# Scaling after the experts instead of before: rounded parts of x1, tokens on partitions, in a one-core MetaFormer block

## The reference

```
x = x + attention(layernorm_over_channels(x))          # x: 8 images, 128 channels, 48*48 tokens
t = tokens of x                                        # 128 channels each
logits = layernorm(t) @ gate_w + router_gamma
combine = softmax(logits), only the two largest of 8 kept
mod[e] = gam[e] * (layernorm(t) @ expert_w[e] + expert_b[e]) + bet[e]
t = t + sum over e of combine[e] * mod[e]
```

## Time and profile before

| | |
|---|---|
| median of three runs (lowest to highest) | 736.78 us (733.86 to 740.26) |
| profiled execution, its own time | 737.64 us |
| its span, first to last instruction | 735.9 us |
| busy TensorE / weight loads / VectorE | 681.8 / 458.9 / 632.3 us |
| busy ScalarE / GpSimd | 292.0 / 468.7 us |
| mean granted TensorE clock | 0.978 |

### The profile page before, as it was taken

The page is one execution under the profiler, slowest core; times in us unless marked ns, Lnnn a source line. Parts: engine busy times, 40 slices in busy tenths (PEclk is TensorE's granted clock), DMA queues, the critical chain, the costliest instruction groups (busy, mean ns, idle before and its releaser), DMA issues.

```text
span 735.9 us, 35372 instructions
## 1 busy us (share of the span) xinstructions
PE 681.8 (93%) x13757; PEld 458.9 (62%) x13865; DVE 632.3 (86%) x1690; ACT 292.0 (40%) x865; POOL 468.7 (64%) x696
## 2 busy tenths in 40 slices
PE   3667999989999999999999999999999999999986
PEld 1656656656666666666666666666666666665542
DVE  3667999988999999999999999999999999988762
ACT  1134434433444444444444444444444444434311
POOL 5365765565667676767676767676767676764521
PEclk9788999999999999999999999999999999999997
DMA  4111111111111111111111111111111111011000
GB/s 109 53 35 32 45 32 46 46 45 32 45 43 43 43 43 43 43 43 43 43 43 42 44 42 43 42 44 42 44 42 43 42 43 41 29 31 33 17 17 29
DMA packets 60229, 30.53 MB, mean 41 GB/s; under 512 B 2160, under 2 KB 60176, under 8 KB 60176
## 3 DMA queue, kind: packets, MB, share of 16 engines
q1 hardware_dynamic: 60176, 29.79, 14.2%
HBM read 20.34 MB, written 9.44 MB: 40 GB/s over the span
## 4 chain that ended last, share of the span: by engine, by line
PE 82%; issue 8%; POOL 4%; DVE 4%; DMA 1%; ACT 1%; SPq 0%; DVEq 0%; POOLq 0%; ACTq 0%
PE bank_o L1134 31%; PE num L1048 7%; PE num L1031 5%; PE wide_a L1128 4%; PE wide_a L1000 3%; PE num L1015 3%; PE bank_g L1071 3%; PE bank_g L960 3%; PE bank_g L911 3%; PE bank_g L1086 2%; PE bank_g L975 2%; PE wide_a L943 2%; PE bank_o L1093 2%; PE wide_a L945 2%; PE wide_b L943 2%
## 5 line engine op out<-in xcount | busy, mean ns | idle before, releaser
L1134 PE MATMUL bank_o<-xs,e_w 128*128 128x512 f32 x576 | 279.7, 610 | 0.2 <-DVE xs L774 0.2
L1134 PEld LDWEIGHTS bank_o<-xs,e_w 128*128 128x128 f32 x576 | 99.3, 191 | 88.0 <-issue 87.5
L338 POOL TENSOR_TENSOR qn<-feat,rden 128x512 f32<-128x512 f32 x36 | 38.8, 1077 | 114.0 <-DVE rden L654 114.0
L374 POOL TENSOR_TENSOR xs<-spread,x 128x1024 f32<-128x1024 f32 x36 | 97.7, 2714 | 4.4 <-ACT spread L498 4.4
L774 DVE TENSOR_TENSOR xs<-wide_a,x 128x1024 f32<-128x1024 f32 x72 | 87.5, 1215 | 6.2 <-PE wide_b L1128 6.1
L456 ACT ACTIVATE q_eo<-bank_g,parity 128x512 f32<-128x512 f32 x72 | 45.5, 683 | 96.3 <-PE bank_g L975 96.3
L465 ACT ACTIVATE squares<-bank_g 128x128 f32<-128x128 f32 x108 | 28.5, 274 | 137.3 <-issue 70.0
L326 POOL TENSOR_TENSOR k_sum<-k_sum,feat 128x64 f32<-128x64 f32 x216 | 68.8, 318 | 16.9
L637 DVE SCALAR_TENSOR_TENSOR feat<-ex,qkv 128x512 f32<-128x512 f32 x72 | 79.3, 1103 | 0.0
L366 POOL TENSOR_TENSOR coef<-weight,coef 128x256 fp32r<-128x256 f32 x36 | 26.1, 724 | 83.0 <-ACT coef L486 83.0
L307 POOL TENSOR_TENSOR x_low<-x,x_high 128x512 fp32r<-128x512 f32 x36 | 61.1, 1697 | 4.6 <-ACT x_high L421 4.6
(11 more groups left out here) (161 smaller groups left out, 1630.7 us busy)
## 6 DMA issues: line engine op xcount, KB each, us to landing
x<-in_x SPq DMA_DIRECT2D x36, 256.0 KB, 2.9
x_res<-in_x SPq DMA_DIRECT2D x36, 256.0 KB, 2.9
...
```

The lines of the kernel that those rows point to most:

```text
L374: tt(xs[:, g.par, 2 * pair:2 * pair + 2], spread[:], flat(x1[:, g.par]).unsqueeze(1) .broadcast_to([128, 2, U * T]), ALU.mult).then_inc(S[ ...
L1134: last = mm(bank_o[:], e_w[:, e], xs[:, g.par, e], start=False, stop=(final and e % 2 == 1), skip_group_check=True)
```

## The change

The experts no longer read scaled copies of `x1`. ScalarE rounds `x1` to `x1_high`, GpSimd takes the rest `x1_low`, and `experts(g, u, half)` makes, for one image and four experts, three fp32r matmuls of 512 columns with the tokens as the stationary operand: the result has tokens on partitions and four experts side by side in a bank. Since tokens are on partitions, an expert's weight for a token is a per-partition scalar: ScalarE scales experts 5 to 8 into `part` (`scaled_by_scalar`), GpSimd adds these in pairs to `two_sums` (`add_parts`), and VectorE multiplies and adds experts 1 to 4 onto the first sum in `total` (`experts_1_to_4`). TensorE's `output` puts the bias rows, the transposed `two_sums` and the transposed `total` into `bank_o`. One transpose of `pack` replaces four of `coef4`. `spread_scales`, `scale_pair`, `spread_pair`, `sel` and `e_w` are gone; the expert weights are centred and split (`e_high`, `e_low`).

The set-up is cut up: the first images are transposed ahead of `first_weights`, and the rest of it stands inside the first steps (`if first(g)`). GpSimd's fills of `v_pad`, `state` and others pass to VectorE. SyncE loads the second images ahead of the small weights, stores at age 9 instead of 7 and loads the residual at age 4 instead of 3. The steps of all engines are in a new order.

The core of the diff:

```diff
+        weight = sb("weight", [128, U, EXPERTS])
+        scale = sb("scale", [128, PAR, U, EXPERTS])
+        pack = sb("pack", [128, U, 2, 2, EXPERTS], F32R)
         coef_t = sb("coef_t", [128, PAR, U * T], F32R)
-        spread = sb("spread", [128, 2, 512])
-        xs = sb("xs", [128, PAR, EXPERTS, U * T])
+        part = sb("part", [128, U, 4, 128])
+        two_sums = sb("two_sums", [128, PAR, U, 2, 128])
+        total = sb("total", [128, PAR, U, 128])
         o = sb("o", [128, PAR, U, T])
...
                 g = at(0)
                 if g:
                     load_later(g)
-                g = at(7)
+                g = at(9)
                 if g:
                     store(g)
-                g = at(3)
+                g = at(4)
                 if g:
                     load_residual(g)
 
-            steps(sp, step, 7)
...
+            def x1_low_part(g):
+                need(pool, "x1_high_done", g.i + 1)
+                need(pool, "a_2", g.i - 1)
+                tt(x1_low[:, g.par], x1[:, g.par], x1_high[:, g.par].bitcast(F32), ALU.subtract)\
+                    .then_inc(S["x1_low_done"], 1)
+
+            def add_parts(g, p):
+                need(pool, f"part{2 * p}", g.i + 1)
+                need(pool, f"part{2 * p + 1}", g.i + 1)
                 need(pool, "out_done", g.i - 1)
-                tt(xs[:, g.par, 2 * pair:2 * pair + 2], spread[:], flat(x1[:, g.par]).unsqueeze(1)
-                   .broadcast_to([128, 2, U * T]), ALU.mult).then_inc(S[done], 1)
+                two = slice(2 * p, 2 * p + 2)
+                tt(two_sums[:, g.par, two], part[:, two, 0:2], part[:, two, 2:4], ALU.add).then_inc(S[f"two_sums{p}"], 1)
...
+            def x1_high_part(g):
+                need(act, "x1_done", g.i + 1)
+                need(act, "a_2", g.i - 1)
+                need(act, "x1_low_done", g.i - 1)
+                nc.scalar.activation(x1_high[:, g.par], x1[:, g.par], copy).then_inc(S["x1_high_done"], 1)
+
+            def scaled_by_scalar(g, u):
+                need(act, "scale_done", g.i + 1)
+                need(act, f"two_sums{u // 2}", g.i)
+                need(act, f"b_{u}", g.i + 1)
+                for e in range(4):
+                    last = nc.scalar.activation(part[:, u, e], w_bank[B_BANK[u]][:, 128 * e:128 * e + 128], copy,
+                                                scale=scale[:, g.par, u, 4 + e:5 + e])
+                last.then_inc(S[f"part{u}"], 1)
...
-                nc.scalar.activation(spread[:].rearrange("p n t -> p (n t)"), bank[:], copy).then_inc(S[done], 1)
+                need(act, "out_done", g.i - 1)
+                for u in range(U):
+                    rows = slice(ROWS * u, ROWS * u + ROWS)
+                    last = nc.scalar.activation(coef_t[rows, g.par, T * u:T * u + T], bank_g[rows, 0:T], copy)
...
+            def expert_weights():
                 for e in range(EXPERTS):
-                    make(nc.vector.tensor_scalar(e_w[:, e], w_bank[e // 4][:, 128 * (e % 4):128 * (e % 4) + 128],
-                                                 gamma_all[:, e:e + 1], None, ALU.mult))
-                dve.wait_ge(S["rest_pe"], 3)
-                make(stt(e_bias[:], e_bias_raw[:], gamma_col[:], num[0:EXPERTS, 256:384], ALU.mult, ALU.add))
-                dve.wait_ge(S["rest_pe"], 4)
-                make(copy(eb_high[:], num[:, 640:768]))
-                dve.wait_ge(S["rest_dve"], done[0])
-                make(tt(eb_low[:], num[:, 640:768], eb_high[:].bitcast(F32), ALU.subtract))
-                dve.wait_ge(S["rest_dve"], done[0])
-                make(tt(eb_rows[:], num[:, 512:640], eb_low[:], ALU.add))
-                assert done[0] == REST_DVE
-                dve.wait_ge(S["rest_dve"], REST_DVE)
+                    make(nc.vector.tensor_scalar(e_high[:, e], e_centred[:, e], gamma_all[:, e:e + 1], None, ALU.mult))
+                dve.wait_ge(S["rest_dve"], BIASES + EXPERTS)
+                for e in range(EXPERTS):
+                    make(stt(e_low[:, e], e_centred[:, e], gamma_all[:, e:e + 1], e_high[:, e].bitcast(F32),
+                             ALU.mult, ALU.subtract))
...
-                tt(weight[:, :, 0], weight[:, :, 1], per_token(rstd2[:, g.par]), ALU.mult).then_inc(S["scale_done"], 1)
-
-            def scale_pair(g, pair, spread_done, done):
-                need(dve, spread_done, g.i + 1)
-                need(dve, "x1_done", g.i + 1)
+                need(dve, "part0", g.i - 1)
+                need(dve, "part1", g.i - 1)
+                need(dve, "part2", g.i - 1)
+                need(dve, "part3", g.i - 1)
+                tt(scale[:, g.par], weight[:], per_token(rstd2[:, g.par]), ALU.mult).then_inc(S["scale_done"], 1)
+
+            def experts_1_to_4(g, p):
                 need(dve, "out_done", g.i - 1)
-                tt(xs[:, g.par, 2 * pair:2 * pair + 2],
-                   (wide_a, wide_b)[pair % 2][:].rearrange("p (n t) -> p n t", n=2),
-                   flat(x1[:, g.par]).unsqueeze(1).broadcast_to([128, 2, U * T]), ALU.mult).then_inc(S[done], 1)
+                need(dve, f"two_sums{p}", g.i + 1)
+                need(dve, "scale_done", g.i + 1)
+                need(dve, f"a_{2 * p}", g.i + 1)
+                need(dve, f"a_{2 * p + 1}", g.i + 1)
+                done = S[f"a_steps{p}"]
+                for e in range(4):
+                    for k in range(2):
+                        u = 2 * p + k
+                        if e > 0:
+                            dve.wait_ge(done, 6 * g.i + 2 * e - 1 + k)
+                        before = total[:, g.par, u] if e > 0 else two_sums[:, g.par, u, 0]
+                        last = stt(total[:, g.par, u], w_bank[A_BANK[u]][:, 128 * e:128 * e + 128],
+                                   scale[:, g.par, u, e:e + 1], before, ALU.mult, ALU.add)
+                        if e < 3:
+                            last.then_inc(done, 1)
+                last.then_inc(S[f"a_sum{p}"], 1)
 
...
+                    features(g, 0)
+                    if first(g):
+                        gammas_and_gate()
 
             first_weights()
-            rest_of_weights()
             steps(dve, step, 6)
...
+            def experts(g, u, half):
+                if first(g):
+                    pe.wait_ge(S["rest_dve"], REST_DVE)
+                need(pe, "x1_low_done", g.i + 1)
+                if (u, half) == (0, 0):
...
-                    last = mm(bank_o[:], e_w[:, e], xs[:, g.par, e], start=False, stop=(final and e % 2 == 1),
+                        need(pe, "a_sum1", g.i)
+                        need(pe, "part3", g.i)
+                out, four = w_bank[(A_BANK, B_BANK)[half][u]], slice(4 * half, 4 * half + 4)
+                mm(out, x1_high[:, g.par, u], e_high[:, four], start=True, stop=False)
+                mm(out, x1_high[:, g.par, u], e_low[:, four], start=False, stop=False)
+                mm(out, x1_low[:, g.par, u], e_high[:, four], start=False, stop=True).then_inc(S[f"{'ab'[half]}_{u}"], 1)
+
+            def output(g):
+                if first(g):
+                    pe.wait_ge(S["rest_dve"], REST_DVE)
+                need(pe, "a_sum0", g.i + 1)
+                need(pe, "a_sum1", g.i + 1)
+                need(pe, "squares_done", g.i + 2)
+                need(pe, "lg_done", g.i + 2)
+                if g.edge:
+                    need(pe, "o_done", g.i)
+                need(pe, "ct_evac", g.i + 1)
+                mm(bank_o[:], eb_rows[:], coef_t[:, g.par], start=True, stop=False, skip_group_check=True)
+                for u in range(U):
+                    out = bank_o[:, T * u:T * u + T]
+                    mm(out, two_sums[:, g.par, u, 1], ident[:], start=False, stop=False, is_transpose=True,
+                       skip_group_check=True)
+                    last = mm(out, total[:, g.par, u], ident[:], start=False, stop=(u == U - 1), is_transpose=True,
                               skip_group_check=True)
-                if final:
-                    last.then_inc(S["out_done"], 1)
+                last.then_inc(S["out_done"], 1)
...
                 g = at(3)
                 if g:
-                    key_values(g)
+                    if first(g):
+                        gammas_and_gate()
+                    k_transposed(g)
+                g = at(4)
+                if g:
+                    from_state(g)
                 g = at(0)
                 if g:
                     x_transposed(g)
-                g = at(4)
-                if g:
-                    scores(g)
-                g = at(6)
-                if g:
-                    experts(g, 3, "scaled3", True)
+                    if first(g):
+                        first_weights()
+                g = at(5)
+                if g:
...
-            first_weights()
-            rest_of_weights()
```

623 lines of the change are left out of this document (330 added, 293 removed).

## The result

| | before | after |
|---|---|---|
| median (lowest to highest) | 735.63 us of 4 runs (733.86 to 740.26) | 686.53 us of 4 runs (684.97 to 688.55) |
| profiled execution, its own time | 737.64 us | 687.47 us |
| ratio after to before | | 0.9325, 95% interval 0.9272 to 0.9378 |

The change makes the kernel 6.75% faster. The forecast was 707 us, 4% less; the measured gain of 49 us is more than half as much again as the forecast 30. Some executions of a kernel are slower, at a lower granted clock; the medians take in all of them, the ratios leave these out.

What follows compares the result with a forecast made beforehand. TensorE and VectorE were both taken as full, with VectorE setting the round after the change. 79 filling + 29 x 18.1 + 98 draining + 3.3 = 705, plus 1.74: 707 us against 737.64; range 686 to 744.

Steps and rivals of the forecast that it cites:

- Two engines are full: Middle 400 us: TensorE busy 99%, VectorE 93%, so relieving TensorE alone would uncover VectorE.
- VectorE's round: VectorE's work per round: 17.77 - 3.4 + 4.2 - 0.6 = 17.97 us; the whole round forecast at 18.1.
- early ones hold a collision: Early rounds before: VectorE's features read 2.89 us beside GpSimd's product, so 29 rounds average 18.75, more than 18.21.
- the tight spot before the masked scores: TensorE's way to the scores 6.4 us against VectorE's 6.5: no slack, 0.1 to 0.2 added per round.
- The multiply-adds: VectorE, 16 per round on 128 elements, 0.26 us each, 4.2 together; upper bound 0.38 each, 6.1.
- The 512-column matmuls: TensorE, 24 rounded ones per round at 0.235 us, 5.6 together; other bound 0.43 each, 10.3.
- The loop: Second pair of `total`, router, `scale`, ScalarE's batches, GpSimd's sum, next second pair: 17.7 us, 0.3 below VectorE's 17.97.
- Filling: Time to first output: 88.8 - 14 (earlier start) + 4.4 (set-up work inside rounds) = 79 us.
- Draining: The last six rounds, 100.0 us before, forecast at 98.
- The features did not meet GpSimd's sums: Rival, no gain in the rounds: features meet GpSimd's sums each round, 0.3 to 0.7 us; 716 to 727 us, chance 0.17.
- VectorE did not wait before the masked scores: Rival, slower: VectorE waits for TensorE's scores, 8.0 us against 6.5, round 19.6, 750 us; chance 0.08.
- More gain: Rival: multiply-adds at 0.2 us, round 17.3 bounded by the loop, 684 us; chance 0.08.

Runs made afterwards that it cites:

- experiments 2 and 3: Kernel before without two of eight expert matmuls: 728.06 us; the same with GpSimd's product also cut from 1024 to 64 columns: 698.40 us.
- experiment 5: Changed kernel without the matmuls on the low part of the expert weights (8 of 24 per round): median 693.24 us, ratio 0.9353.
- experiment 6: Changed kernel without VectorE's multiply-adds of expert 4 (4 of 16 per round): 675.35 us, ratio 0.9190, round 17.10.
- experiment 4: Changed kernel with the whole set-up ahead of the first step again on TensorE and VectorE: 698.87 us, ratio 0.9483, first output at 96.4.
- experiment 12: Changed kernel with VectorE's variances ahead of `x1` and its four statistics instructions in gaps between router instructions: 695.11 us, ratio 0.9424.
- experiment 10: Changed kernel with variances ahead of `x1`, key-value masks and projections 3 and 2 ahead of the second pair of `total`: 812.16 us, ratio 1.1046.

## Why the prediction was right in sign and short in size

**The limits.** "Two engines are full, and relieving TensorE alone uncovers VectorE" is right: experiments 2 and 3.

**VectorE's round, the step that failed.** The prediction takes "17.77 us of it is work, short gaps between dependent instructions included". 0.66 of it was waiting: the second features instruction behind GpSimd's product. I saw this collision in the early rounds and put it down to them ("early ones hold a collision"); in the round that I read line by line, its row, 401.08 with 1.32, was taken for the length of the instruction. The row beside it in the same timeline, 0.69 for the same instruction on the same shape, said otherwise. Line by line against that round, the measured 17.46 follows from 18.1 with: 0.66 less for the features, 0.12 less for the variances, 0.09 less for scaling the projections, 0.13 less for the tight spot before the masked scores, where nothing waits, 0.21 more for the wait that is left behind the residual and 0.11 more for `den1` and `rden`. That gives 17.42; the missing 0.04 are the multiply-adds, whose 4.21 hold the hidden wait of 0.08. The new order makes the features start 0.15 after the sum; that the collision was avoided is due to this and to the missing product. The prediction had not worked out the 0.15; that part is luck.

**The multiply-adds**, forecast at 0.26 each and 4.2 together, took 4.21, the wait included. The router's gaps gave 0.59 for a forecast 0.6.

**TensorE.** The 512-column matmuls stand 0.23 apart, forecast 0.235 (TensorE, timeline):

```profile
413.58 0.39 PE L1214 MATMUL wide_a<-e_high,x_low 128*128 128x512 f32 x1
413.81 0.39 PE L1212 MATMUL wide_a<-e_high,x_high 128*128 128x512 f32 x1
414.04 0.39 PE L1213 MATMUL wide_a<-e_low,x_high 128*128 128x512 f32 x1
```

The eight transposes into the output bank start 0.11 apart, as forecast. TensorE's 96% is no bound (experiment 5).

**ScalarE and the loop.** Eight copies in 2.02, 0.25 each, forecast 0.29; four pieces of coefficients in 1.09, forecast 0.8:

```profile
415.46 2.17 ACT L497 ACTIVATE part<-wide_a,scale 128x128 f32<-128x128 f32 x8
417.48 1.09 ACT L515 ACTIVATE coef_t<-bank_g 32x128 fp32r<-32x128 f32 x4
```

The loop was forecast at 17.7 (its terms add up to 17.6) and measures 17.57 in the round shown, 17.46 on average. I took it for 0.3 below VectorE's round. VectorE's work came down to 17.38, below the loop, and so the loop sets the round now (experiment 6).

**Filling.** 79 was forecast and 79.4 came, by luck: experiment 4 gives the place of the set-up 17.0 (forecast 14), so the rest costs 7.6 (forecast 4.4), and the two errors cancel. The images are transposed at 4.00 and the first projection starts at 14.11, where before the first transposes were at 26.19 (TensorE, timeline):

```profile
4.00 1.12 PE L975 MATMUL bank_g<-ident,x 128*128 128x128 f32 x4 [4.00 <-DMA x<-in_x]
...
14.11 0.67 PE L1005 MATMUL wide_b<-w_high,x_high 128*128 128x384 f32 x1
```

**Draining**, forecast at 98, took 90.3. The forecast counted the end of the chain and left out that each of the six rounds shortens too: the first four went from 70.7 to 65.9, the last two from 29.3 to 24.4. What took 4.9 from the last two, where 2 were counted, no run here takes apart.

The sum of what was missed: 29 x 18.1 - 512.6 = 12.3 in the rounds, 98 - 90.3 = 7.7 in the draining, 0.4 and 0.1 the other way at the two ends: 19.5, which is 707 - 687.5. The 12.3 are 14.0 in the 22 steady rounds, less 1.7 in the first seven, which hold the rest of the set-up and took 18.34 each.

**The rivals.** The features did not meet GpSimd's sums in the steady rounds of the changed order, though they do in experiment 12, where they stand half a microsecond earlier against the sum. VectorE did not wait before the masked scores; experiment 10 shows the mechanism in another order. "More gain" came, bounded by the loop as it said, but not by shorter multiply-adds.
